# Eight gated experts of the last layer, worked for the two chosen per token through lists in HBM instead of for all tokens

## What is computed

```python
x = x + ctx @ Wo                                   # first half: 16-head attention
m = _layernorm(x, ln2_g, ln2_b)
xt = m.reshape(-1, Dd)                             # 2048 x 128
probs = jax.nn.softmax(xt @ Wg, axis=-1)           # 8 experts
wts, idx = jax.lax.top_k(probs, K)                 # K = 2
wts = wts / jnp.sum(wts, axis=-1, keepdims=True)
h1 = jax.nn.gelu(jnp.einsum('td,edf->etf', xt, W1) + b1[:, None, :])   # 128 -> 512
ye = jnp.einsum('etf,efd->etd', h1, W2) + b2[:, None, :]               # 512 -> 128
sel = ye[idx, jnp.arange(T)[:, None], :]
moe_out = jnp.sum(wts[..., None] * sel, axis=1).reshape(Bb, Ss, Dd)
return x + moe_out
```

## Time and profile before

| | us |
|---|---|
| median of 3 runs | 2380.46 (2379.5 to 2381.55) |
| the profiled execution's own time | 2369.72 |
| its span, first to last instruction | 2367.9 |
| PE busy in the span | 2005.6 (85%) |
| DVE busy | 1526.4 (64%) |
| ACT busy | 998.5 (42%) |
| POOL busy | 721.7 (30%) |
| mean granted TensorE clock | 0.929 of full speed |

### The profile page before, as it was taken

How to read it: one execution, slowest core, us unless ns; L and a number is a source line. 1 busy time by engine, 2 the same in 40 slices (tenths; PEclk the granted TensorE clock), 3 DMA queues, 4 the chain that set the end, 5 groups by cost and what they waited for, 6 DMA issues and landing times.

```text
span 2367.9 us, 50631 instructions
## 1 busy us (share of the span) xinstructions
PE 2005.6 (85%) x20823; PEld 1278.5 (54%) x20823; DVE 1526.4 (64%) x3477; ACT 998.5 (42%) x2428; POOL 721.7 (30%) x917
## 2 busy tenths in 40 slices
PE   6679999999797899967778999999998454779998
PEld 3325556565545565426575666666665122447776
DVE  5799985878756655478417776766655998871101
ACT  3536654666537322323134555555542001334342
POOL 2244544555505242043304100000005652421111
PEclk9879999999999999978798999999999776899998
DMA  9000001000063001500340110000000000000000
GB/s 376 9 1 1 1 1 67 4 5 5 29 277 130 2 1 72 232 2 2 132 132 23 37 28 19 10 19 18 10 1 1 9 9 18 2 2 1 1 1 19
DMA packets 37015, 100.96 MB, mean 43 GB/s; under 512 B 11120, under 2 KB 22078, under 8 KB 30128
## 3 DMA queue, kind: packets, MB, share of 16 engines
q1 hardware_dynamic: 35760, 95.84, 11.1%
q0 software_dynamic: 1024, 1.88, 0.3%
HBM read 91.08 MB, written 6.85 MB: 41 GB/s over the span
## 4 chain that ended last, share of the span: by engine, by line
PE 54%; DVE 28%; issue 8%; ACT 7%; POOL 1%; DMA 1%; SPq 0%; POOLq 0%; DVEq 0%; ACTq 0%
PE PS L2240 6%; PE PS L3646 5%; PE PS L2440 3%; PE PS L416 3%; PE PS L3103 3%; PE PS L3093 2%; PE PS L3151 2%; PE PS L452 2%; PE PS L360 2%; DVE arena L1731 2%; DVE arena L246 2%; PE PS L3143 1%; DVE arena L3559 1%; ACT arena L3215 1%; PE PS L3135 1%
## 5 line engine op out<-in xcount | busy, mean ns | idle before, releaser
L313 POOL TENSOR_TENSOR arena<-arena 128x4 f32<-128x4 f32 (+2 forms) x101 | 115.7, 1146 | 840.3 <-DVE arena L257 403.7
L3215 ACT ACTIVATE arena<-PS,arena 128x289 f32<-128x289 f32 x256 | 127.0, 506 | 176.7 <-DVE arena L3320 173.4
L2240 PEld LDWEIGHTS PS<-arena 128*128 128x128 f32 x1408 | 167.5, 192 | 33.4 <-issue 33.4
L2254 DVE TENSOR_TENSOR arena<-PS,arena 128x512 f32<-128x512 f32 x64 | 44.3, 693 | 201.5 <-PE PS L2240 197.6
L2240 PE MATMUL PS<-arena 128*128 128x128 f32 x1408 | 167.9, 275 | 1.5 <-DVE arena L2509 1.5
L360 PE MATMUL PS<-arena 128*128 128x512 f32 x298 | 160.1, 654 | 5.9 <-DVEq L3783 4.2
L2260 POOL TENSOR_TENSOR arena<-arena 128x512 f32<-128x512 f32 x68 | 79.8, 1174 | 274.2 <-DVE arena L2254 255.6
L1795 POOL TENSOR_TENSOR arena<-arena 128x128 f32<-128x128 f32 x384 | 140.6, 405 | 47.8 <-PE PS L1658 23.0
L3683 ACT ACTIVATE arena<-PS,arena 128x512 f32<-128x512 f32 x128 | 88.0, 687 | 128.9 <-PE PS L3646 128.9
L3103 PE MATMUL PS<-arena 128*128 128x289 f32 x512 | 136.1, 409 | 2.3 <-DVE arena L3314 1.7
L1731 DVE RECIPROCAL arena<-PS 128x128 f32<-128x128 f32 x96 | 91.7, 955 | 48.6 <-PE PS L1696 48.2
(11 more groups left out here) (366 smaller groups left out, 4781.0 us busy)
## 6 DMA issues: line engine op xcount, KB each, us to landing
arena<-in_ctx SPq DMA_DIRECT2D x48, 1090.0 KB, 7.8
arena<-in_f_w SPq DMA_DIRECT2D x32, 256.0 KB, 3.0
arena<-in_ctx SPq DMA_DIRECT2D x16, 512.0 KB, 3.9
arena<-in_late SPq DMA_DIRECT2D x1, 7316.0 KB, 21.2
arena<-in_mid SPq DMA_DIRECT2D x1, 3796.5 KB, 11.6
arena<-in_w SPq DMA_DIRECT2D x1, 3017.0 KB, 13.4
slots_in<-arena SPq DMA_DIRECT2D x1, 1280.0 KB, 5.5
slots_out<-arena SPq DMA_DIRECT2D x16, 80.0 KB, 1.7
```

The costliest lines, as they stand in the source:

```text
L313: e.tensor_tensor(x, x, half.broadcast_to(list(x.shape)), ALU.pow).then_inc(*T.done("norm_root", tag))
L2240: k = e.matmul(PS[:, b, D * j:D * j + D], hT[:, f, P * j:P * j + P], self.down(x, f), start=f == 0, stop=f == self.n_hidden - 1)
L3215: e.activation(self.weights(n, k, 0, UL), PS[:, k, 0:UL], ACT.Exp, bias=self.st[:, h, k:k + 1], accum_out=self.st[:, h, 4 + k:5 + k]).then ...
```

## The change

The second half of `L3Ffn` works only the two chosen experts of each token.

- **Choice and place.** Per quarter, `pick` (DVE) finds the two largest logits and counts, `locate` (PE) and `spot` (DVE) give each token two places in lists by expert; the region of expert x begins at row 2048x of the HBM tensor `lists`. The two gates come from one exponential of the difference.
- **Scatter.** POOL writes rows of 130 words (128 normalised features, the gate, and the place of the answer) by 32 indirect DMAs of 128 rows. `lists` was filled with blanks by SP during the attention (8 DMAs of 1040 KB and one of 65 KB); a blank's answer place lies out of bounds.
- **Tiles.** `tile_list` makes the numbers of the 39 tiles of 128 rows that can be needed (unused ones point to a blank tile). SP reads each number into a register, loads that expert's weights (`f3_w`, 128 x 1028 words, 526 KB) and the tile's rows (67 KB), through rings of 6. PE turns the rows, makes hidden and down parts (1 + 4 + 4 matmuls of 128x128), ACT applies gelu, DVE moves the turned rows and multiplies by the gate, and POOL scatters 128 answers of 512 B to `answers`.
- **End.** When the last four scatters have landed, SP loads `answers` back in 8 DMAs of 256 KB and DVE adds them to `g.X`, 8 adds of 128x512.
- **Around it.** The bias part `f3_b` moves ahead of the tiles, followed by 14 filler matmuls. The layer's expert weights leave the load `in_late`. In the attention half POOL gets a fill of 128x2080 words and three small operations, DVE one small fill and two casts of 128x128.

```diff
+    TILES = (2 * NTOK - E) // P + E
+    WIDTH = F + 4 * D + 4
+    RING = 6
...
+        def weights(k):
+            for w in T.due(("f3_down", k - self.RING)):
+                e.wait_ge(*w)
+            at = e.value_load(self.list[0:1, k:k + 1], min_val=0, max_val=NT * E)
+            x = g.nc.s_assert_within(at >> 4, 0, E)
+            e.dma_start(self.w[k % self.RING], t["f3_w"][bass.DynSlice(x, 1)].rearrange("a p f -> (a p) f")).then_inc(
+                *T.done(f"f3_weights{k % self.RING}", (k, 0), 16))
+            return at
+
+        def rows(k, at):
+            j = k - self.RING
+            for w in T.due(("f3_rows_out", j), (f"f3_gathered{j % 4}", j)):
+                e.wait_ge(*w)
+            e.dma_start(self.x[k % self.RING], lists[bass.DynSlice(at, 1)].rearrange("a p w -> (a p) w")).then_inc(*T.done(*self.loaded(k), 16))
...
+        ahead = [weights(k) for k in range(3)]
+        for w in T.due(("f3_scattered", 2 * NT - 1)):
+            e.wait_ge(*w)
+        for k in range(self.TILES):
+            rows(k, ahead[k] if k < 3 else weights(k))
...
-        x_ = self.experts
-        for n, (x, q) in enumerate(x_.places):
...
+        idle_pe(e, T, g, free, 6, 14)
+        turn(0)
+        for k in range(self.TILES + 2):
+            if k + 1 < self.TILES:
+                turn(k + 1)
+            if k < self.TILES:
+                hidden(k)
+            if k >= 2:
+                down(k - 2)
...
+        norm_pool(e, T, g, "f3_m", self.small, qs=range(3))
+        scatter(0)
+        norm_pool(e, T, g, "f3_m", self.small, qs=(3,))
+        for q in range(1, NQ):
+            scatter(q)
+        for k in range(self.TILES):
+            at = self.x[k % self.RING][:, D + 1:D + 2].bitcast(mybir.dt.uint32)
+            for w in T.due(("f3_rows_out", k)):
+                e.wait_ge(*w)
+            e.indirect_dma_start(t["answers"][:, :], bass.IndirectOffsetOnAxis(ap=at, axis=0), self.y[k % 4], None,
+                                 bounds_check=2 * NTOK - 1, oob_is_err=False).then_inc(*T.done(f"f3_gathered{k % 4}", k, 16))
...
+        stats(0)
+        stats(1)
+        rows(0)
+        rows(1)
+        self.pick(e, T, 0)
+        stats(2)
+        self.spot(e, T, 0)
+        rows(2)
+        self.pick(e, T, 1)
+        stats(3)
+        self.spot(e, T, 1)
+        rows(3)
+        self.pick(e, T, 2)
+        self.spot(e, T, 2)
+        self.pick(e, T, 3)
+        self.spot(e, T, 3)
+        self.tile_list(e, T)
+        for q in range(NQ):
+            self.gates(e, T, q)
```

More of the change, by code:

```diff
@@ L3602, in __init__ @@
                                 g.XT, float(1.0 / np.sqrt(np.float32(HD))), self.OT)
[L3604 to L3610, removed]
+        self.fill = room.take(NT, self.ROW)
@@ new lines, in __init__ @@
+        self.top, self.first, self.place = [room.take(4) for _ in range(2)], room.take(4), room.take(4, E)
+        self.ex, self.den, self.slotf = room.take(NT), room.take(4), room.take(4)
+        self.slot = [room.take(NT).bitcast(I32) for _ in range(2)]
+        self.count, self.tiles, self.end, self.skip = (room.take(1, parts=E) for _ in range(4))
+        self.full, self.past = room.take(NT, parts=E), room.take(self.TILES, parts=E)
+        self.listf, self.list = room.take(self.TILES, parts=1), room.take(self.TILES, parts=1).bitcast(I32)
@@ L3651, in pe, with route, locate @@
[L3651 to L3654, removed]
+        def route(q):
+            cols_pe(e, T, g, "f3_m", self.rows[0][:, :, 0:D], free, range(4), qs=(q,))
+            free[q] = ("cols_act", ("f3_m", q))
+            rows_pe(e, T, g, "f3_r", g.XT, W["f3_Wg"], q, 4 + q, free, [("cols_act", ("f3_m", q))], ("f3_logit", q))
+        def locate(q):
+            at = slice(4 * q, 4 * q + 4)
+            for w in T.due(free[q], ("f3_counts", q)):
+                e.wait_ge(*w)
+            e.matmul(g.PS[:, q, 0:4 * E], self.upto, self.both[:, at], start=True, stop=False)
+            e.matmul(g.PS[:, q, 0:4 * E], self.ones, self.runh[:, at], start=False, stop=True).then_inc(*T.done("f3_located", q))
+            free[q] = ("f3_place", q)
@@ new lines, in pe @@
+        route(0)
+        route(1)
+        locate(0)
+        route(2)
+        locate(1)
+        route(3)
+        locate(2)
+        locate(3)
+        for name, out, left, right, before in (("count", g.PS[0:E, 4, 0:1], self.run[:, NT, :], C["ones"][:, 0:1], ("f3_counts", NQ - 1)),
+                                               ("end", g.PS[0:E, 4, 0:1], C["upto"][0:E, 0:E], self.tiles, ("f3_tiles", 0)),
+                                               ("list", g.PS[0:1, 4, 0:self.TILES], self.skip, self.past, ("f3_past", 0))):
+            for w in T.due(free[4], before):
+                e.wait_ge(*w)
+            e.matmul(out, left, right, start=True, stop=True).then_inc(*T.done("f3_located", name))
+            free[4] = (f"f3_{name}", 0)
@@ new lines, in turn, with hidden @@
+        def turn(k):
+            b = k % 2
+            for w in T.due(free[b], self.loaded(k)):
+                e.wait_ge(*w)
+            e.transpose(g.PS[:, b, 0:P], self.x[k % self.RING][:, 0:D], C["ident"]).then_inc(*T.done("f3_turned", k))
+            free[b] = ("f3_sT_dve", k)
+        def hidden(k):
+            b = 2 + k % 2
+            for w in T.due(free[b], ("f3_sT_dve", k)):
+                e.wait_ge(*w)
+            for f in range(4):
+                i = e.matmul(g.PS[:, b, P * f:P * f + P], self.w[k % self.RING][:, P * f:P * f + P], self.xT[k % 2], start=True, stop=True)
+            i.then_inc(*T.done("f3_hidden", k))
+            free[b] = ("f3_gelu", k)
```

305 lines of the change are left out of this document (228 added, 77 removed).

## The result

The changed kernel takes 2347.89 us, median of 4 runs (2342.64 to 2352.1); beside them the kernel before takes 2379.98 (4 runs, 2377.32 to 2381.55). The ratio is 0.9865, 95% interval 0.9841 to 0.9889: faster by 32 us. I had forecast 71.5 us less and 2309. The direction and the range held; more than half of the gain did not come.

A forecast was written before the change was run, and what follows sets the result against it. PE was taken to bound the experts, 224 us for 32 places. With choice and scatter, 39 tiles at 2.5 us and a 15.2 us end, the last add moves from 2362.35 to 2290.8: 71.5 us less, 2309.0, range 2285 to 2350.

The forecast's parts named there:

- the ring of 6: Tile stage: rows k load only after scatter k-6 lands; 5.6 us behind a down part, giving 2.27 to 2.53 a tile.
- 1.3 to landing: Tile stage: an answer scatter lands 1.3 us after POOL's part of it, a figure taken from layer 8.
- T: Time from tile to tile over the 39 tiles, taken as 2.5 us, between 2.13 and 2.9.
- The DMA bound: Tile stage: 657 KB a tile at 309 GB/s takes the DMA engines 2.13 us.
- the rival in which SP paces: Tile stage: SP or the loads set 2.9 to 3.7 us a tile, 2324 to 2355 us in all; chance 0.20.
- Costed at nothing: POOL's fill, DVE's fill and casts, and SP's 8.4 MB of blanks in the attention half lie hidden in waits: 0 us.
- Choice, places and scatter: Last layer's second half, before the tiles: list at 2150.3, last list scatter ends 2162.3, rows landed at 2165.6.
- Bias pairs and fillers: PE ahead of the tiles: four pairs at 3.75 us, fillers 14.12 us; first tile at 2180.1, 14.5 us after the data.
- The end: From last down part to last add: scaling, scatter, landing, 2 MB of answers loaded, last two adds; 15.2 us, uncovered.
- PE pacing: Rival, tile stage: the ring hides everything, 2.0 to 2.15 us a tile, 2285 to 2291 us in all; chance 0.14.
- PE at the lower level through the tiles: Rival: PE's clock stays low, 0.52 us a matmul, 4.7 a tile, 2392 us; a mixture 2328 to 2366; chance 0.07.
- Transfers that don't overlap: Rival, in the ring: loads pass one after another, 6.5 us a tile, 2461 us, slower than before; chance 0.05.

The follow-up runs named there:

- Experiment 4: The changed kernel with weights loaded only for the first six tiles, later tiles reusing what stands in the buffers: 2313.0 us, one execution.
- experiment 2: The changed kernel with 12 instead of 6 buffers for the rows of a tile, weights keeping 6: 2311.78 us, ratio 0.9739.
- experiment 6: The changed kernel with 12 row and 9 weight buffers, no fillers, and the bias pairs behind the last tile: 2284.41 us, ratio 0.9617.
- experiment 1: The kernel before with only POOL's fill and SP's nine blank stores added: 2378.84 us beside 2375.55, ratio 1.0016.
- experiment 10: The kernel before with the fill and only the 65 KB blank, none of the eight 1 MB stores: 2374.04 us, ratio 0.9995.
- experiment 11: The kernel of experiment 6 with the blank stores held until the averages of the last head block but one: 2282.2 us, ratio 0.9595.
- experiment 3: The changed kernel without the 14 filler matmuls ahead of the first tile: 2331.11 us, ratio 0.9814.
- experiment 5: The changed kernel with 12 row buffers and 9 weight buffers in place of 6 each: 2299.44 us, ratio 0.9674.
- 7: The kernel of experiment 6 with the eight 1 MB blank stores spread over the attention heads: 2282.73 us, ratio 0.9606.
- 12: The kernel of experiment 11 with the four bias pairs ahead of the tiles again: 2280.9 us beside 2373.71, ratio 0.9615.

## Why the prediction was right or wrong, by its steps

**The step that failed is the ring of 6**, in it the term "1.3 to landing". The mechanism was right: a loop over three tiles through rows buffer, scatter and load sets T for most of the stage. Its sum was 5.6 + 2.0 = 7.6 us for three tiles. Measured around 2228 it is 0.36 + 0.71 (DVE and the way to POOL) + 0.97 (POOL) + 3.42 (landing) + 0.20 (SP) + 1.74 (load) + 3.54 (PE, partly at a lower clock), with the gaps between 11.1. The landing alone is 2.1 over, 0.7 us a tile. PE's 1.5 over are of hops like this one, where its clock is down; in the hop at 2246 its share is 2.14. My 2.6 for the row load was 0.9 too high, which hid some of the miss. Not every scatter lands so late: the nine on the chain up to 2291 land 1.7 to 3.6 us behind POOL's end, 2.8 on average. I had taken the 1.3 from the last scatter of layer 8, beside which no load was under way; the last one of the tiles, behind which nothing more was being loaded, also took only 2.08 from its start:

```profile
2328.74 2.08 DMA answers<-arena
```

Experiment 4 gives 1.5 behind POOL's end without the weight loads, and T 2.51; experiment 2 takes the ring away and leaves the loads, and T is 2.49. Either one alone removes 0.66 to 0.68 us a tile, 25 to 26 us over the 38, and with it PE's loss to its clock, which is 1.00 in the tiles of both. My text named this among what would make it wrong ("scatters that take over 4 us to land under load") and gave it no price.

**PE's share** was right: 9 matmuls in 1.89 us at full clock against 2.0. **The DMA bound** of 2.13 was too high. It came from 309 GB/s in the earlier trace rows; experiment 6 moved 349 GB/s at a share of 0.99, 1.88 us for 657 KB. Here the share at part load did not scale to the rate at full load: the three windows of the changed kernel's tiles would give 290 to 309 GB/s.

**The register load**, for which I had bounds of 0 and 1.7 us, is small (ns, min/median/max):

```profile
L3655 SPq TENSOR_LOAD <-arena x39: 5/267/564, 2170.9 to 2315.5; - x39
```

With the register operations, the two issues of 0.33 and the gaps between, SP needs 1.7 us a tile where nothing holds it up, here from one row load to the next (L3665, the weight load L3657 between):

```profile
2223.45 0.33 SPq L3665 DMA_DIRECT2D arena<-lists  x1
2224.59 0.33 SPq L3657 DMA_DIRECT2D arena<-in_f_w  x1
2225.16 0.33 SPq L3665 DMA_DIRECT2D arena<-lists  x1
```

That is below every T that was measured, so the rival in which SP paces did not occur; its range of T did, by another cause. But it is close to the 1.9 of the fastest versions, where SP has little to spare. The Trainium skill (DMA: Bandwidth & Descriptors, "Latency and other measured facts") gives such a load a floor of about 600 ns; none of the 39 here reached it.

**Costed at nothing, wrongly: the blanks.** Their price was 3.3 us of median (experiment 1), 3.5 to 6 in the profiles. I had shown that the transfer fits into the 60 us of heads and that nobody waits for it, and both are so. What I had not asked is what else uses the same DMA engines: PE's instruction packets do. The fill was free, as said (experiment 10). So were DVE's fill and casts: in experiment 11, which has them and moves the blanks elsewhere, the attention half takes 92.8.

**Choice, places and scatter** held in their parts. The eight scatters ahead of the root of quarter 3 make DVE wait 2.5 us, scatters follow at 1.28, and SP's first row load is issued 1.5 us behind the last scatter's end (1.3 forecast). The first tile came 76.7 and 76.5 us after the last add in experiments 2 and 4, against 75.9 forecast. In the profiled execution it came 84.1. There DVE has waits that the others lack:

```profile
2167.50 0.18 DVE L3913 RECIPROCAL arena<-arena 128x4 f32<-128x4 f32 x1 [2.36 <-remote]
...
2180.68 0.69 DVE L4012 TENSOR_TENSOR arena<-PS,arena 128x512 f32<-128x512 f32 x1 [4.86 <-remote]
```

The first, with shorter ones of 0.3 to 1.1 us in the 10 us ahead of it and one of 1.0 behind, makes the list 8.3 us later than forecast, and the bias pairs and fillers behind it with it; the second lies beside the pairs.

**Bias pairs and fillers** cost what I said: the pairs 15.8 us at the lower level (15.0 forecast), the fillers 13.6 (14.1), both on the path. That the data was there 14.5 us earlier stood in the prediction as a remark; experiment 3 shows that it was 12 us to be had.

**The end** took 16.1 against 15.2.

**The rivals.** PE pacing: only with both rings larger. PE at the lower level through the tiles: in part. The clock was 0.90, 0.97 and 0.88 in tiles with PE idle 0.3 of the time, and 1.00 in experiment 6 where it never waits. The Trainium skill's account that I had named (TensorE: Matmul & The Clock Gate, "HAM oscillation") is of loops whose compute is shorter than their wait. Here the compute was the longer in every run, and the changed kernel still lost some clock; experiments 2 and 4 have 1.00 with PE busy 0.8 of the time, so a wait for a load in each loop need not cost any. Transfers that don't overlap: no. Loads of 65 and 526 KB reached 349 GB/s, so the Trainium skill's rule on sizes under 1 MiB (DMA: Bandwidth & Descriptors, "Rules for kernel authors"), read as a cost that is paid in series, would have misled here: with the buffers to keep many under way, small ones fill the engines.

Experiment 2 gives 2311.8, where I had 2309, with T = 2.49 where the forecast's average was 2.37. That they meet so closely is partly luck: in experiment 2 the weights' ring and SP set T, a limit that I had not summed, and the blanks' 3 us were not in my sum.

## What to carry to other kernels

- A loop through a ring of buffers is priced with every member at its duration under the loads that run beside it. If the trace shows the member only in a quiet stretch, that number is the lower bound; take buffers for more than it. With one ring out of the way, price the next one: here that of the weights. Here six more row buffers of 520 bytes a partition were worth 30 us, and three more for weights another 15.
- Work on the engine that comes next (fillers, pairs) belongs where that engine would wait anyway. When the data is there, as here, they are the delay. That fillers of 14 us are free when the data is late by 14 us is the other side of it, which no run here shows.
- A transfer that nobody waits for can still cost, when it fills the DMA engines for long. A place for it is beside a stretch that issues few instructions (experiment 11), where 1 to 2 us of it were left by the profile; the medians can't tell that gain from none.

## What was not expected of the hardware

- PE idles in mid-group, with no semaphore to wait for, up to 2.9 us at a time while 8.6 MB of stores hold the DMA engines at a share of 0.99 to 1.01, and up to 3.6 us with 17 MB (1.01 to 1.02). Each time a 16 KB packet of kind instruction has come late, and PE goes on 1.2 to 1.6 us behind its end. The cost goes with the bytes, not with how they are spread: 3.3 us for 8.6 MB in a burst or in eight pieces, about 11 for 17 MB.
- An indirect scatter of 64 KB lands 1.1 to 1.8 us behind POOL's end with no weight load beside it, and 1.7 to 3.6 behind it when loads of 526 KB run beside it, one per 3.2 us. Of the eleven row loads of 65 KB on the changed kernel's chain seven took 1.7 to 2.1 us and four 2.4 to 4.1.
- Between the choice and the first tile, several engines are held up at once in some executions, with nothing to wait for in the code: DVE at small operations for 1.6 to 4.9 us at a time (ended by "remote", an event whose sender the profile does not show), and SP at its first weight loads. Its three issues take 2.7 us where this is absent, and with it this much:

```profile
2158.36 9.50 SPq L3662 DMA_DIRECT2D arena<-in_f_w  x3
```

  That row is of experiment 6, in which the first rows were asked for 3.6 us behind the last scatter's end instead of 1.5, and so the first tile came 4 us later than I had expected. Such waits are in five of the nine profiles of kernels with the choice of two (the changed kernel, experiments 5, 6, 7 and 12), in none of the other four (2, 3, 4 and 11), with the same code around them. Each begins while POOL's scatters to `lists` run. Experiment 11 has a milder form: waits of 0.5 to 1.2 us on DVE, and one of 2.9 on POOL. What causes them stays open. Counted from the last add, the fillers of experiment 5 end 13 us later than those of experiment 2, which has no such waits; they may be part of why runs of one of these kernels differ by 5 to 19 us, which no run shows.
